# Fifteen stages on one core: constants loaded in the first norm, semaphores cleared in the next stage, output by chunk, rows of a partition side by side

## The chip, the cores and the metric

The kernel runs on one core of a Trainium2 chip. The metric is device time in microseconds (us) of one execution. The median of three runs of the kernel before is 4643.16 us (4641.54 to 4646.2).

## What is computed

4096 tokens of 128 features go through four layers, each with an attention (or a mixing) part and a feed-forward part. Every part adds to the same residual, and a layer norm stands ahead of each layer. Cut to its shape:

```python
def _layernorm(x, axis=-1, eps=1e-05):
    m = jnp.mean(x, axis=axis, keepdims=True)
    v = jnp.var(x, axis=axis, keepdims=True)
    return (x - m) / jnp.sqrt(v + eps)
...
act = jax.nn.silu(hpre)
y = jnp.einsum('tef,efh->teh', act, W2) + b2
out = jnp.einsum('te,teh->th', cw, y)
```

Layer 0 has softmax attention with 16 heads, a second attention block, and 8 dense experts. Layer 1 has attention with rotary tables and 8 experts of which each token takes 2. Layer 2 has linear attention and 8 experts with 2 for each token and a fixed capacity of 1024 rows for each expert. Layer 3 is a recurrent mixing and 64 small experts of which each token takes 8.

## The kernel before, in words

The residual `res_t` and the normed input `xn_t` stay in SBUF, features on the 128 partitions, tokens along the free side, in 8 chunks of 512 columns (`CH`, `BANK`). The program (`program`, L2950 on) is a row of 15 stages, each a function with one `Block`: n0, a0, b0, r0, e0, then n1, r1, a1, e1, then n2, r2, a2, e2, then n3, m3 (n is `layer_norm`, a an attention, b `whole_attention`, r a routing, e the experts, m `mixing_and_experts`). A `Block` gives each engine its own list of instructions and ends with a barrier: every engine drains, then all wait for one another. Within a block semaphores alone set the order.

Five places matter here.

The first block of `program` (L2955) is SP's alone: it issues the DMA of `avg`, of the eight chunks of `x` (L2961), and of 20 further constants (L2964). Norm n0 is the next block. Its tensor engine waits for `avg`, for each chunk of `x` and, ahead of the last chunk, for all the constants (`kept_in`).

At the end of every stage `pl.close()` (L39) opens one more `Block`, in which SP clears the stage's semaphores one by one (L45), and the barrier of that block has the line L41.

After the last stage a block of its own stores the output, one DMA of 2 MB, and waits for it (L3003, L3006).

The experts of layers 1 and 2 (`sorted_experts`, e1, and `slot_experts`, e2) read tokens that an earlier stage has scattered to DRAM by expert, 130 floats (520 bytes) to a row. Spans of 512 rows (e1) or 1024 rows (e2) are loaded with row t*128+p on partition p (L2753, L2513). The products go back to DRAM by indirect DMA, 128 rows of 512 bytes each, at the row numbers that travel with the tokens (L2865, L2642). In the end `y_in` is loaded in 16 DMAs of 256 KB (L2759, L2534), turned and added by the tensor engine (L2816, L2817; L2593, L2594), and added to the residual by the vector engine. A table `dest2` gives each token the row j*4096 + token.

In e2 SP's order is: weights, bias, a wait for the scatter, slots of expert 0 and 1, then the reloads. POOL (GpSimd) issues all the indirect DMAs.

Of the kernel before, what the change touches and what calls it, by code (L numbers as in the profile page):

```python
# [14 lines left out]
P = 128  # L15
# [7 lines left out]
class Place:  # L23


    def __init__(self, nc, ctx, stage):
        self.nc, self.ctx, self.stage, self.sems = nc, ctx, stage, []
# [7 lines left out]
    def sem(self, name):  # L35
        self.sems.append(self.ctx.enter_context(self.nc.semaphore(f"{self.stage}_{name}")))
# [25 lines left out]
def layer_norm(nc, stage, res_t, xn_t, avg, ident, bias, arrived=()):  # L62
# [6 lines left out]
    with ExitStack() as ctx:  # L69
# [87 lines left out]
def wide_attention(nc, stage, res_t, xn_t, w_d, w_out_d, ident, rowmask, scale, eps, clears, cleared):  # L157
# [41 lines left out]
    with ExitStack() as ctx:  # L199
# [319 lines left out]
def small_attention(nc, stage, res_t, xn_t, w, wo, ident, less, rope, w_moe_d, b_moe_d, split_d, split_out,  # L519
# [53 lines left out]
    with ExitStack() as ctx:  # L573
# [42 lines left out]
        with nc.Block() as block:  # L616
            @block.sync
            def _(eng):
                eng.wait_ge(filled, 3)
# [246 lines left out]
def whole_attention(nc, stage, res_t, xn_t, xp_t, w, bias, ident):  # L866
# [33 lines left out]
    with ExitStack() as ctx:  # L900
# [32 lines left out]
        with nc.Block() as block:  # L933
            @block.tensor
# [119 lines left out]
def linear_attention(nc, stage, res_t, xn_t, w_d, w_out_d, mask, ident, eps, rows, slot_of, slots_d, cleared, cleared_count, scattered):  # L1054
# [15 lines left out]
    with ExitStack() as ctx:  # L1070
# [49 lines left out]
        with nc.Block() as block:  # L1120
            @block.sync
            def _(eng):
                for p in range(PAIRS):
                    eng.dma_start(w[:, p, :], w_d[p, :, :]).then_inc(w_in, 16)
                    if p == 0:
                        eng.dma_start(wo[:, :, :], w_out_d).then_inc(const_in, 16)
                    eng.wait_ge(w_in, 16 * (p + 1))
                eng.wait_ge(const_in, CONSTS)

# [186 lines left out]
def route(nc, stage, x_t, w, bias, tri, ident, gates_d, E, top, norm_eps, squash, extra, extra_value, capacity):  # L1316
# [10 lines left out]
    with ExitStack() as ctx:  # L1327
# [37 lines left out]
        with nc.Block() as block:  # L1365
            @block.sync
            def _(eng):
                eng.wait_ge(turned_free, CH)
                eng.dma_start(gates_d, gates_t[:, :]).then_inc(stored, 16)
                eng.wait_ge(stored, 16)  # L1370
# [123 lines left out]
def mixing_and_experts(nc, stage, res_t, xn_t, d, gates_d, w_d, ident, w_route):  # L1494
# [49 lines left out]
    with ExitStack() as ctx:  # L1544
# [102 lines left out]
        with nc.Block() as block:  # L1647
            @block.sync
            def _(eng):
                for n in shape:  # L1650
                    eng.dma_start(const[n][tuple(slice(None) for _ in shape[n])], d[n + "3"]).then_inc(const_in, 16)
                eng.dma_start(w[:, :, :], w_d[0, :, :, :]).then_inc(w_in, 16)

# [6 lines left out]
                for n in range(UNITS):  # L1660
                    for pair in range(CH // 2):
# [394 lines left out]
def experts(nc, stage, res_t, x_t, w_d, bias_d, gates_d, units, act):  # L2056
# [42 lines left out]
    with ExitStack() as ctx:  # L2099
# [28 lines left out]
        with nc.Block() as block:  # L2128
            @block.sync
            def _(eng):  # L2130
# [9 lines left out]
                load_side(1, 1)  # L2140

# [131 lines left out]
def dispatch(nc, stage, xn_t, w, tri, ident, dest, base, rows, slot_of, norm_eps, sort, w_row):  # L2273
# [4 lines left out]
    with ExitStack() as ctx:  # L2278
# [34 lines left out]
        with nc.Block() as block:  # L2313
            @block.tensor
# [135 lines left out]
def slot_experts(nc, stage, res_t, slots_d, y_d, w_d, bias_d, ident, filled_sem, filled_count, sent):  # L2450
# [11 lines left out]
    with ExitStack() as ctx:  # L2462
# [44 lines left out]
        with nc.Block() as block:  # L2507
            @block.sync
            def _(eng):
                def load_slots(e):  # L2510
                    if e >= RING:
                        eng.wait_ge(gated, PER * (e - RING + 1))
                    eng.dma_start(slots[:, e % RING, :, :], slots_d[e * CAPACITY:(e + 1) * CAPACITY, :].rearrange("(t p) c -> p t c", p=P)).then_inc(slots_in[e % RING], 16)  # L2513
# [7 lines left out]
                eng.dma_start(bias[:, :, :], bias_d.rearrange("e p j -> p e j")).then_inc(const_in, 16)  # L2521
                eng.wait_ge(filled_sem, filled_count)
# [163 lines left out]
def sorted_experts(nc, stage, res_t, xn_t, slots_d, y_d, split_d, w_row, ident, filled_sem, filled_count, w_in, sent):  # L2686
# [9 lines left out]
    with ExitStack() as ctx:  # L2696
# [49 lines left out]
        with nc.Block() as block:  # L2746
            @block.sync
            def _(eng):
                eng.wait_ge(filled_sem, filled_count)
                for s in range(SORTED):  # L2750
                    if s >= SR:
                        eng.wait_ge(gated, s - SR + 1)
                    eng.dma_start(slots[:, s % SR, :, :], slots_d[s * BANK:(s + 1) * BANK, :].rearrange("(t p) c -> p t c", p=P)).then_inc(slots_in[s % SR], 16)  # L2753
                for r in range(2):
                    eng.wait_ge(sent[r], 16 * TILES * ((SORTED + 1 - r) // 2))
                for c in range(CH):
                    for j in range(2):
                        rows = slice(j * T + c * BANK, j * T + (c + 1) * BANK)
                        eng.dma_start(y_in[:, j, TILES * c:TILES * (c + 1), :], y_d[rows, :].rearrange("(t p) c -> p t c", p=P)).then_inc(y_loaded[c], 16)  # L2759
# [165 lines left out]
def program(nc, d, out):  # L2925

    gates = nc.dram_tensor("gates", (SMALL_EXPERTS + 2, T), F32, kind="Internal").ap()
    with ExitStack() as ctx:
# [20 lines left out]
                ("avg", "ident", "bias0", "rowmask0", "w_b0", "bias_b0", "w_g0", "b_g0", "tri", "dest2", "base2", "sort1", "w_g1", "w_qkv1",  # L2949
# [5 lines left out]
        with nc.Block() as block:  # L2955
            @block.sync
            def _(eng):
# [4 lines left out]
                for n in kept:  # L2962
                    if n != "avg":
                        eng.dma_start(kept[n][tuple(slice(None) for _ in d[n].shape)], d[n]).then_inc(kept_in, 16)  # L2964

        def in_parts(to, source, rows):
# [8 lines left out]
                   arrived=[([(avg_in, 16)] if c == 0 else []) + [(x_in[c], 16)] + ([(kept_in, 16 * (len(kept) - 1))] if c == CH - 1 else []) for c in range(CH)])  # L2975
# [25 lines left out]
        mixing_and_experts(nc, "m3", res_t, xn_t, d, gates, d["w_small"], kept["ident"], kept["w_route"])  # L3001

        with nc.Block() as block:  # L3003
            @block.sync
            def _(eng):
                eng.dma_start(out, res_t[:, :]).then_inc(stored, 16)  # L3006
                eng.wait_ge(stored, 16)


def lay_out(a):  # L3010
# [53 lines left out]
    def side_by_side(w, shared):  # L3064
# [22 lines left out]
        "w_g2": a["L2_ffn_gate_w"].T, "slots1": slots1, "sort1": sort1, "slots2": slots2, "dest2": ((np.arange(2) * T)[None, :, None] + np.arange(NT)[None, None] * P + p[:, :, None]).astype(np.float32),  # L3087
# [25 lines left out]
```

## Time and profile before

| | |
|---|---|
| median of the runs | 4643.16 us (4641.54 to 4646.2) |
| the profiled execution | 4609.9 us, with a span of 4607.5 us |
| TensorE busy | 4042.7 us, 88% of the span |
| VectorE busy | 3472.0 us, 75% |
| ScalarE busy | 2982.6 us, 65% |
| GpSimd busy | 2365.3 us, 51% |

Times are microseconds from the start of the span. PE is the tensor engine's matmul, PEld its weight load, DVE the vector engine, ACT the scalar engine, POOL GpSimd, SP the engine that issues most DMAs. A q behind an engine's name means its instruction queue: barriers, semaphore instructions and DMA issues, which aren't counted as busy. The profiled execution is 33 us shorter than the median of the runs; what lies around its span is 2.4 us.

### The profile page before, as it was taken

What the parts mean: (1) busy time and instruction counts of PE and PEld (TensorE: products, weight loads), DVE (VectorE), ACT (ScalarE), POOL (GpSimd) and SP (SyncE); (2) the same over time, 40 slices, a digit from 0 to 9 for tenths busy, and PEclk for the clock granted to TensorE, in tenths of its full rate; (3) what the DMA queues carried; (4) which work ended last, traced back from release to release, by engine and by line L of the source; (5) the groups of instructions that cost most, each with busy time, mean ns of one, the idle gap of its engine ahead of it and who ended that gap; (6) DMA issues with size and microseconds to landing.
All of it is one profiled execution on the core that took longest, in us unless ns stands there. A gap on an engine that the chain in (4) does not pass through costs nothing. (4 is left out here: it accounts for less than half of the span.)

```text
span 4607.5 us, 88670 instructions
## 1 busy us (share of the span) xinstructions
PE 4042.7 (88%) x34700; PEld 2257.5 (49%) x34700; DVE 3472.0 (75%) x4781; ACT 2982.6 (65%) x4498; POOL 2365.3 (51%) x1443
## 2 busy tenths in 40 slices
PE   5999999999998989985877777896888869999998
PEld 2666666666676644441111211344777443444443
DVE  5888888888884557756889898574777747888888
ACT  2777777777775459952677777782665726555564
POOL 2888888888884013320221110461666526666665
PEclk7999999999999989985899999897999979999999
DMA  2122212221120011100120100340000333333342
GB/s 81 45 51 57 57 42 51 57 57 48 48 48 1 1 70 46 69 1 28 62 73 31 43 22 13 109 138 26 13 14 13 102 92 94 95 100 99 95 105 75
DMA packets 139405, 261.47 MB, mean 57 GB/s; under 512 B 23908, under 2 KB 71908, under 8 KB 137388
## 3 DMA queue, kind: packets, MB, share of 16 engines
q1 hardware_dynamic: 123572, 215.01, 17.2%
q0 software_dynamic: 15424, 40.89, 2.6%
q8 instruction: 271, 4.44, 0.4%
q14 instruction: 138, 1.13, 0.1%
HBM read 170.31 MB, written 49.76 MB: 48 GB/s over the span
## 5 line engine op out<-in xcount | busy, mean ns | idle before, releaser
L513 POOL TENSOR_TENSOR a_prob_low<-a_prob_whole,a_prob_high 128x1024 f16<-128x1024 f32 x512 | 1084.9, 2130 | 276.6 <-ACT a_prob_high L403 276.6
L487 DVE TENSOR_REDUCE a_part_max<-a_top 128x2 f32<-128x1024 f32 x512 | 626.1, 1223 | 218.6 <-PE a_top L314 212.6
L400 ACT ACTIVATE a_prob_whole<-a_score 128x1024 f32<-128x1024 f32 x512 | 525.3, 1026 | 332.4 <-PE a_score L303 320.4
L757 ACT ACTIVATE a_prob<-a_score 128x512 f32<-128x512 f32 x1024 | 533.0, 603 | 260.7 <-PE a_score L701 260.7
L789 DVE TENSOR_REDUCE a_part_max<-a_side 128x2 f32<-128x1024 f32 x512 | 595.1, 1219 | 86.3 <-PE a_side L672 86.3
L1920 POOL TENSOR_TENSOR m_scaled<-m_acted,m_gate 128x512 f32<-128x512 f32 x264 | 433.2, 1649 | 271.5 <-DVE m_acted L2038 201.6
L403 ACT ACTIVATE a_prob_high<-a_score 128x1024 f16<-128x1024 f32 x512 | 521.9, 1019 | 0.0
L302 PE MATMUL a_score<-a_qa,a_ka 128*128 128x256 f16 x2048 | 476.2, 273 | 0.0
L303 PE MATMUL a_score<-a_qb,a_kb 128*128 128x256 f16 x2048 | 476.1, 273 | 0.0
L369 PE MATMUL a_o_ps<-a_v,a_prob_high 128*128 128x65 f16 x4096 | 428.1, 193 | 6.3 <-POOL a_prob_low L513 3.4
L371 PE MATMUL a_o_ps<-a_v,a_prob_high 128*128 128x64 f16 x4096 | 426.9, 194 | 0.0
L373 PE MATMUL a_o_ps<-a_v,a_prob_low 128*128 128x65 f16 x4096 | 424.5, 192 | 0.0
L369 PEld LDWEIGHTS a_o_ps<-a_v,a_prob_high 128*128 128x128 f16 x4096 | 376.0, 96 | 85.7 <-DVE a_tokens L473 35.3
L371 PEld LDWEIGHTS a_o_ps<-a_v,a_prob_high 128*128 128x128 f16 x4096 | 377.7, 97 | 26.9 <-issue 10.9
L373 PEld LDWEIGHTS a_o_ps<-a_v,a_prob_low 128*128 128x128 f16 x4096 | 377.9, 98 | 0.0
L1871 ACT ACTIVATE m_acted<-m_up_down 128x512 f32<-128x512 f32 x264 | 157.4, 597 | 320.7 <-PE m_up_down L1700 320.0
L701 PE MATMUL a_score<-a_qa,a_ka 32*128 32x512 f16 x1024 | 238.5, 400 | 91.0 <-ACT a_prob L757 88.4
L713 PE MATMUL a_o_ps<-a_prob,a_v 128*32 128x512 f32 x2048 | 290.4, 641 | 13.8 <-ACT a_raw L746 13.7
L701 PEld LDWEIGHTS a_score<-a_qa,a_ka 32*128 32x128 f16 x1024 | 60.4, 92 | 435.7 <-ACT a_prob L757 367.2
L2256 DVE TENSOR_TENSOR e_low<-e_whole,e_high 128x512 f16<-128x512 f32 x256 | 212.5, 842 | 80.3 <-ACT e_high L2214 79.9
L672 PE MATMUL a_side<-a_ka,a_qa 32*128 32x512 f16 x1024 | 217.9, 403 | 44.6 <-DVE a_part_max L789 22.3
L2044 DVE TENSOR_TENSOR m_lows<-m_scaled,m_high 128x512 f16<-128x512 f32 x264 | 241.8, 916 | 5.1 <-ACT m_high L1879 5.0
(440 smaller groups left out, 10378.0 us busy)
## 6 DMA issues: line engine op xcount, KB each, us to landing
m_gate<-gates SPq DMA_DIRECT2D x264, 256.0 KB, 5.1
a_ka<-a_nat_high_k SPq DMA_DIRECT2D x128, 128.0 KB, 2.4
e_gate<-gates SPq DMA_DIRECT2D x8, 2048.0 KB, 7.0
slots<-in_slots SPq DMA_DIRECT2D x19, 520.0 KB, 4.1
a_qa<-a_nat_high_q SPq DMA_DIRECT2D x64, 128.0 KB, 2.4
a_qa<-a_nat_low_q SPq DMA_DIRECT2D x64, 128.0 KB, 2.4
a_qb<-a_nat_high_q SPq DMA_DIRECT2D x64, 128.0 KB, 2.4
a_kb<-a_nat_low_k SPq DMA_DIRECT2D x64, 128.0 KB, 2.4
```

Source lines behind the costliest of these rows:

```text
L302: eng.matmul(score[:, e % 2, h, i, :], ka[:, r, h, keys], qa[:, r, h, qs], start=True, stop=False)
L303: mm = eng.matmul(score[:, e % 2, h, i, :], kb[:, r, h, keys], qb[:, r, h, qs], start=False, stop=True)
L369: eng.matmul(o_ps[:, at:at + V1], high, v[:, r, kt, h, 0:V1], start=(pair == 0 and i == 0 and h == 0 and t == 0), stop=False, skip_group_c ...
L371: eng.matmul(o_ps[:, at:at + DH], high, v[:, r, kt, h, V1 + 1:VW], start=False, stop=False, skip_group_check=True)
L373: mm = eng.matmul(o_ps[:, at:at + V1], low, v[:, r, kt, h, 0:V1], start=False, stop=last, skip_group_check=True)
L400: eng.activation(prob_whole[:, e % RING, :, :, :], score[:, e % 2, :, :, :], ACT.Exp, scale=scale)
L403: eng.activation(prob_high[:, e % RING, :, :, :], score[:, e % 2, :, :, :], ACT.Exp, scale=scale).then_inc(exp_done, 1)
L487: eng.tensor_reduce(part_max[:, i, c, :, qt % 4], top[:, :, :], AX.X, ALU.max).then_inc(max_done, 1)
L513: eng.tensor_tensor(prob_low[:, e % RING, :, :, :], prob_whole[:, e % RING, :, :, :], prob_high[:, e % RING, :, :, :], ALU.subtract).then_ ...
L757: eng.activation(prob[:, e % RING, h, :], score[:, step % SLOTS, :], ACT.Exp).then_inc(exp_done, 1)
L789: op = eng.tensor_reduce(part_max[:, qt // 4, c, 2 * pair:2 * pair + 2, 24 + qt], side, AX.X, ALU.max)
L1920: eng.tensor_tensor(scaled[:, s % SR, :], acted[:, s % AR, :], gate[:, g % 2, j, c % 2 * BANK:(c % 2 + 1) * BANK], ALU.mult).then_inc(scal ...
```

## The change

The kernel after differs in four ways.

1. The first block issues only `avg` and `x`. The 20 other constants are issued by SP inside the block of n0 (`loads`), with `bias0` ahead of `ident`.
2. `close()` opens no block. A stage's semaphores are kept until the next stage, whose SP clears them (`clear_before`): at the head of its list in the norms, b0, the routings and a1; behind the loads of weights in a0 and a2; behind the first loads in e0 and m3; behind weights and bias and ahead of the first slots in e2; behind the second load of slots in e1. The semaphores of m3 aren't cleared.
3. The last block is gone. In m3 SP stores each chunk of the output when its last two additions are done, and waits for all eight.
4. Loads of slots and of `y_in` take the rows of a partition side by side ("(p t) c" for "(t p) c"), and `dest2` gives token t*128+p the row p*32+t.

```diff
     def close(self):
-
-        with self.nc.Block() as block:
-            @block.sync
-            def _(eng):
-                for s in self.sems:
-                    eng.sem_clear(s)
+        if Place.before:
+            Place.before.held.close()
+        Place.before = self
...
+    def clear_before(self, eng):
+        for s in Place.before.sems if Place.before else ():
+            eng.sem_clear(s)
...
         with nc.Block() as block:
+            @block.sync
+            def _(eng):
+                pl.clear_before(eng)
+                for to, source in loads:
+                    eng.dma_start(to, source).then_inc(loads_in, 16)
...
+                for c in range(CH):
+                    at = slice(c * BANK, (c + 1) * BANK)
+                    eng.wait_ge(summed, (UNITS - 1) * CH + c + 1)
+                    eng.wait_ge(dve_done, dve_no["res", c])
+                    eng.dma_start(out_d[:, at], res_t[:, at]).then_inc(out_in, 16)
+                eng.wait_ge(out_in, 16 * CH)
...
-                    eng.dma_start(slots[:, e % RING, :, :], slots_d[e * CAPACITY:(e + 1) * CAPACITY, :].rearrange("(t p) c -> p t c", p=P)).then_inc(slots_in[e % RING], 16)
+                    eng.dma_start(slots[:, e % RING, :, :], slots_d[e * CAPACITY:(e + 1) * CAPACITY, :].rearrange("(p t) c -> p t c", p=P)).then_inc(slots_in[e % RING], 16)
...
                 eng.dma_start(bias[:, :, :], bias_d.rearrange("e p j -> p e j")).then_inc(const_in, 16)
+                pl.clear_before(eng)
                 eng.wait_ge(filled_sem, filled_count)
                 load_slots(0)
...
-                        rows = slice(j * T + c * BANK, j * T + (c + 1) * BANK)
-                        eng.dma_start(y_in[:, j, TILES * c:TILES * (c + 1), :], y_d[rows, :].rearrange("(t p) c -> p t c", p=P)).then_inc(y_loaded[c], 16)
+                        rows = y_d[j * T:(j + 1) * T, :].rearrange("(p t) c -> p t c", p=P)
+                        eng.dma_start(y_in[:, j, TILES * c:TILES * (c + 1), :], rows[:, TILES * c:TILES * (c + 1), :]).then_inc(y_loaded[c], 16)
...
-                for n in kept:
-                    if n != "avg":
-                        eng.dma_start(kept[n][tuple(slice(None) for _ in d[n].shape)], d[n]).then_inc(kept_in, 16)
...
-        with nc.Block() as block:
-            @block.sync
-            def _(eng):
-                eng.dma_start(out, res_t[:, :]).then_inc(stored, 16)
-                eng.wait_ge(stored, 16)
+        Place.before.held.close()
+        Place.before = None
+        pl.held.close()
```

## Rows read from the trace of the kernel before

**Rows 1.** The page's first part: busy time of each engine, share of the span, instructions.
```profile
PE 4042.7 (88%) x34700; PEld 2257.5 (49%) x34700; DVE 3472.0 (75%) x4781; ACT 2982.6 (65%) x4498; POOL 2365.3 (51%) x1443
```

**Rows 2.** Start, in order of time: start us, length us, engine, line.
```profile
1.20 3.74 SPq L2961 DMA_DIRECT2D all_res_t<-in_x  x8
...
14.21 0.43 SPq L2964 DMA_DIRECT2D all_kept_w_route<-in_w_route  x1
...
15.23 5.46 PE L102 MATMUL n_mean<-all_res_t,all_kept_avg 128*128 128x512 f32 x6 [15.23 <-PEq L2955]
...
28.38 1.10 PE L102 MATMUL n_mean<-all_res_t,all_kept_avg 128*128 128x512 f32 x2
```

**Rows 3.** Time from issue to landing of x's chunks, and of the last constant.
```profile
DMA to landing us min/median/max: 3.3/4.9/5.8
...
all_kept_w_route<-in_w_route SPq DMA_DIRECT2D x1, 32.0 KB, 4.0
```

**Rows 4.** SP's clears by line: all of them, and those of e2 and of m3.
```profile
L45 SPq EVENT_SEMAPHORE_RANGE_CLEAR  x242: 25/25/49, 47.7 to 4600.6; - x121
...
L45 SPq EVENT_SEMAPHORE_RANGE_CLEAR  x29: 25/25/30, 3730.2 to 3731.8; - x29
...
L45 SPq EVENT_SEMAPHORE_RANGE_CLEAR  x30: 25/30/49, 4598.5 to 4600.6; - x30
```

**Rows 5.** SP's release from e2's own barrier (L2507), then from the clearing block's (L41).
```profile
L2507 SPq EVENT_SEMAPHORE  x1: 17/17/17, 3730.1 to 3730.1; - x1
...
L41 SPq EVENT_SEMAPHORE  x1: 17/17/17, 3732.0 to 3732.0; - x1
```

**Rows 6.** Where clears go: a0's last first-unit load and first score; SP's wait in a1.
```profile
75.08 0.60 SPq L280 DMA_DIRECT2D a_kb<-a_nat_low_k  x1
...
101.96 0.40 PE L302 MATMUL a_score<-a_qa,a_ka 128*128 128x256 f16 x1
...
SPq L623 <- DVE a_fixed L768: 2.3, 1, 2.3
```

**Rows 7.** The end: last addition (chain of waits), last release of SP.
```profile
4597.55 0.69 DVE all_res_t L1941
...
L3003 SPq EVENT_SEMAPHORE  x1: 17/17/17, 4607.5 to 4607.5; - x1
```

**Rows 8.** Issues by line, median us to landing: stores of 256 KB from SBUF to DRAM.
```profile
a_planes<-a_low SPq DMA_DIRECT2D x8, 256.0 KB, 2.1
```

**Rows 9.** e2's start, in order of time.
```profile
3581.54 0.33 SPq L2518 DMA_DIRECT2D e_w<-in_w_moe  x1
...
3582.40 2.57 SPq L2513 DMA_DIRECT2D e_slots<-slots  x2
...
3588.40 1.09 PE L2550 MATMUL e_turned<-all_kept_ident,e_slots 128*128 128x128 f32 x4 [9.23 <-DMA e_slots<-slots]
```

**Rows 10.** e2's end, in order of time.
```profile
3706.46 0.96 POOL L2642 DMA_INDIRECT y<-e_y_s,e_dest  x1 [0.30 <-issue]
3708.77 11.87 SPq L2534 DMA_DIRECT2D e_y_in<-y  x16
3712.28 0.79 PE L2593 MATMUL e_back<-all_kept_ident,e_y_in 128*128 128x128 f32 x2 [19.52 <-DMA e_y_in<-y]
```

**Rows 11.** Tile e_y_in in e1: its loads, and the matmuls that read them.
```profile
L2816 PE MATMUL e_back<-all_kept_ident,e_y_in x64: 273/275/275, 3115.8 to 3129.8; 128*128 128x128 f32 x64
...
L2759 SPq DMA_DIRECT2D e_y_in<-y x16: 359/758/1103, 3096.9 to 3109.1; - x16
```

**Rows 12.** Waits in e1: us in total, times, longest.
```profile
DVE e_y_s L2904 <- DMA y<-e_y_s,e_dest: 31.8, 17, 2.9
```

**Rows 13.** Issues of the scatters, median us to landing.
```profile
y<-e_y_s,e_dest POOLq DMA_INDIRECT x156, 2.6
```

**Rows 14.** Stretches (PE, PEld, DVE, ACT, POOL busy; clock, DMA share, GB/s): x, a0's start.
```profile
7.00:8.00 1.00, 0.00 (x0) 0.00 (x0) 0.00 (x0) 0.00 (x0) 0.00 (x0) 1.00 1.02 377
...
51.00:106.00 55.00, 26.55 (x94) 8.49 (x94) 39.03 (x42) 10.24 (x14) 7.44 (x9) 0.50 0.36 91
```

More of the change, by code:

```diff
@@ L23 @@
 class Place:
+    before = None
     def __init__(self, nc, ctx, stage):
-        self.nc, self.ctx, self.stage, self.sems = nc, ctx, stage, []
+        self.nc, self.ctx, self.stage, self.sems, self.held = nc, ctx, stage, [], ExitStack()
     def sb(self, name, shape, dt=F32):
@@ L35, in sem @@
     def sem(self, name):
-        self.sems.append(self.ctx.enter_context(self.nc.semaphore(f"{self.stage}_{name}")))
+        self.sems.append(self.held.enter_context(self.nc.semaphore(f"{self.stage}_{name}")))
         return self.sems[-1]
+    def clear_before(self, eng):
+        for s in Place.before.sems if Place.before else ():
+            eng.sem_clear(s)
     def close(self):
-        with self.nc.Block() as block:
-            @block.sync
-            def _(eng):
-                for s in self.sems:
-                    eng.sem_clear(s)
+        if Place.before:
+            Place.before.held.close()
+        Place.before = self
 class Steps:
@@ L59, in wait, with layer_norm @@
         eng.wait_ge(self.sem, rnd * len(self.names) + self.place[name])
-def layer_norm(nc, stage, res_t, xn_t, avg, ident, bias, arrived=()):
+def layer_norm(nc, stage, res_t, xn_t, avg, ident, bias, arrived=(), loads=(), loads_in=None):
     LAG = 2
@@ L618, in _ @@
             def _(eng):
+                pl.clear_before(eng)
                 eng.wait_ge(filled, 3)
@@ L933, in whole_attention, with _ @@
         with nc.Block() as block:
+            @block.sync
+            def _(eng):
+                pl.clear_before(eng)
             @block.tensor
@@ L1128, in _ @@
                 eng.wait_ge(const_in, CONSTS)
+                pl.clear_before(eng)
             @block.tensor
@@ L1367, in _ @@
             def _(eng):
+                pl.clear_before(eng)
                 eng.wait_ge(turned_free, CH)
@@ L1491, in route, with mixing_and_experts @@
         pl.close()
-def mixing_and_experts(nc, stage, res_t, xn_t, d, gates_d, w_d, ident, w_route):
+def mixing_and_experts(nc, stage, res_t, xn_t, d, gates_d, w_d, ident, w_route, out_d, out_in):
     GROUPS = 4
@@ L1652, in _ @@
                 eng.dma_start(w[:, :, :], w_d[0, :, :, :]).then_inc(w_in, 16)
+                pl.clear_before(eng)
                 def store(pair):
@@ L2140, in _ @@
                 load_side(1, 1)
+                pl.clear_before(eng)
                 def reload(n, q):
@@ L2313, in dispatch, with _ @@
         with nc.Block() as block:
+            @block.sync
+            def _(eng):
+                pl.clear_before(eng)
             @block.tensor
@@ L2521, in _ @@
                 eng.dma_start(bias[:, :, :], bias_d.rearrange("e p j -> p e j")).then_inc(const_in, 16)
+                pl.clear_before(eng)
                 eng.wait_ge(filled_sem, filled_count)
@@ L2750, in _ @@
                 for s in range(SORTED):
+                    if s == 2:
+                        pl.clear_before(eng)
                     if s >= SR:
                         eng.wait_ge(gated, s - SR + 1)
-                    eng.dma_start(slots[:, s % SR, :, :], slots_d[s * BANK:(s + 1) * BANK, :].rearrange("(t p) c -> p t c", p=P)).then_inc(slots_in[s % SR], 16)
+                    eng.dma_start(slots[:, s % SR, :, :], slots_d[s * BANK:(s + 1) * BANK, :].rearrange("(p t) c -> p t c", p=P)).then_inc(slots_in[s % SR], 16)
                 for r in range(2):
@@ L2757, in _ @@
                     for j in range(2):
-                        rows = slice(j * T + c * BANK, j * T + (c + 1) * BANK)
-                        eng.dma_start(y_in[:, j, TILES * c:TILES * (c + 1), :], y_d[rows, :].rearrange("(t p) c -> p t c", p=P)).then_inc(y_loaded[c], 16)
+                        rows = y_d[j * T:(j + 1) * T, :].rearrange("(p t) c -> p t c", p=P)
+                        eng.dma_start(y_in[:, j, TILES * c:TILES * (c + 1), :], rows[:, TILES * c:TILES * (c + 1), :]).then_inc(y_loaded[c], 16)
             @block.tensor
@@ L2948, in program @@
         kept = {n: pl.sb("kept_" + n, list(d[n].shape)) for n in
-                ("avg", "ident", "bias0", "rowmask0", "w_b0", "bias_b0", "w_g0", "b_g0", "tri", "dest2", "base2", "sort1", "w_g1", "w_qkv1",
+                ("avg", "bias0", "ident", "rowmask0", "w_b0", "bias_b0", "w_g0", "b_g0", "tri", "dest2", "base2", "sort1", "w_g1", "w_qkv1",
                  "w_o1", "less1", "rope", "bias2", "w_g2", "mask2", "w_route")}
@@ L2974, in program @@
         layer_norm(nc, "n0", res_t, xn_t, kept["avg"], kept["ident"], kept["bias0"],
-                   arrived=[([(avg_in, 16)] if c == 0 else []) + [(x_in[c], 16)] + ([(kept_in, 16 * (len(kept) - 1))] if c == CH - 1 else []) for c in range(CH)])
+                   arrived=[([(avg_in, 16)] if c == 0 else []) + [(x_in[c], 16)] + ([(kept_in, 16 * (len(kept) - 1))] if c == CH - 1 else []) for c in range(CH)],
+                   loads=[(kept[n][tuple(slice(None) for _ in d[n].shape)], d[n]) for n in kept if n != "avg"], loads_in=kept_in)
         wide_attention(nc, "a0", res_t, xn_t, d["w_qkv0"], d["w_o0"], kept["ident"], kept["rowmask0"], scale=64 ** -0.5, eps=1e-10,
@@ L3000, in program @@
         layer_norm(nc, "n3", res_t, xn_t, kept["avg"], kept["ident"], None)
-        mixing_and_experts(nc, "m3", res_t, xn_t, d, gates, d["w_small"], kept["ident"], kept["w_route"])
-        with nc.Block() as block:
-            @block.sync
-            def _(eng):
-                eng.dma_start(out, res_t[:, :]).then_inc(stored, 16)
-                eng.wait_ge(stored, 16)
+        mixing_and_experts(nc, "m3", res_t, xn_t, d, gates, d["w_small"], kept["ident"], kept["w_route"], out, stored)
+        Place.before.held.close()
+        Place.before = None
+        pl.held.close()
 def lay_out(a):
```

2 lines of the change are left out of this document (1 added, 1 removed).

## The prediction

> **What bounds the kernel now.** I read the page's first part, then the order of time at every border between stages, then the waits of SP, because the change touches borders and little else. The tensor engine is busy for 88% of the span [rows 1], so only what lies on the chain of waits can shorten it. At a border all engines stand still, and what is removed there counts in full. The reader is to see four borders. At the start nobody works until SP has issued 28 loads [rows 2]. After each stage SP clears semaphores while all the others wait [rows 4, 5]. At the end a store of 2 MB runs alone [rows 7]. In e2 the tensor engine waits for its first slots and for the first rows of y_in [rows 9, 10].
>
> **Constants in the first norm.** The last constant's issue ends at 14.21 + 0.43 = 14.64, and the norm's first matmul starts 0.59 later, at 15.23 [rows 2]. After the change the block ends with x, at 1.20 + 3.74 = 4.94, so the matmul starts at 5.53: 9.7 us earlier. What is late next? Chunk 0 lands 3.3 us after its issue at the soonest row, at 4.5. The eighth chunk, issued at about 4.5 and 5.8 at most on its way, lands at 10.3, and its matmul comes at 28.38 - 9.7 = 18.7 [rows 2, 3]. That matmul also waits for all constants. SP starts on them at about 5.4 in place of 4.94, so the last is issued at about 14.7 and lands 4.0 later, at 18.7 [rows 3]. This is a tie. With x's longest time of 5.8 it would be 1.8 us late. I take 9.7, bounds 7.9 and 9.7. Nothing else stands on SP's queue in the norm.
>
> **Clearing blocks.** There are 242 clears, 30 of them m3's [rows 4], so 212 lie between stages, in 14 blocks. In e2's block 29 clears start over 1.6 us, 0.057 each; from the release of the stage's barrier to that of the clearing block are 1.9 us, and the remaining 0.2 to 0.3 are drain and barrier [rows 4, 5]. 212 x 0.057 + 14 x 0.25 = 15.6 us, all of it on the path, since no engine works there.
>
> The same clears now run on SP beside a stage. In norms, routings and b0, SP has nothing urgent. In a1 they take 8 x 0.057 = 0.5 us ahead of a wait of 2.3 us [rows 6]. In a0 they come ahead of the loads for the first scores, the last of which is issued at 75.08, while the first score comes at 101.96 [rows 6]: 11 x 0.057 = 0.6 us hidden. In a2 nothing of SP follows them. In e0 and m3 they stand behind the first loads, and what follows are reloads and stores that wait for other engines; I take nothing, and where that cover is gone it is 0.5 to 0.6 us each. In e1, 17 clears (1 us) delay the third span of slots, which is used after two whole spans. Only in e2 do they stand on the path: the 20 of a2, 1.1 us, ahead of the slots that the tensor engine waits for [rows 9].
>
> **Output by chunk.** The last addition ends at 4597.55 + 0.69 = 4598.24, the last release is at 4607.5 [rows 7]. Between them lie m3's clears, a barrier and the whole store. After the change only the last chunk's store follows. A store of the same form, 256 KB with 2 KB from each partition, lands in 2.1 us [rows 8]; the upper bound is 4.9, what a chunk of x took amid seven others [rows 3]. With 0.1 to see the semaphore and 0.3 for the last barrier the end is 4600.7: gain 6.8, down to 4.0. The other seven stores run earlier, on a queue with no work behind it. By the Trainium skill, "DMA: Bandwidth & Descriptors", section Bandwidth, transfers should be batched to 1 MiB or more, and this cuts one of 2 MB into eight; it bears on bytes per second, and here only the last piece is on the path, so the sum would not follow it.
>
> **Rows side by side.** In e2 two loads of slots take 2.57 us to issue (1.28 each, runs of 520 bytes), one of weights with runs of 4 KB takes 0.33, and from the first issue to the first turn pass 6.0 us [rows 9]. With runs of 4160 bytes I take a landing of 4.9, the middle row of x [rows 3]: 1.1 gained, and the 1.1 of the clears pays for it. So 0, bounds -1.1 and +1.6 (the 3.3 of x). At e2's end 16 loads are issued in 11.87 us, 0.74 each, and the matmul starts 3.5 us after the first [rows 10]. With 2 KB runs, as x has, an issue takes 3.74 / 8 = 0.47 [rows 2]. The pair is on its way 0.5 us sooner; I take 0.5, bounds 0 and 1. In e1 all of y_in is issued by 3109.1 and used from 3115.8 [rows 11]: nothing. The scatters keep their number and size, and I take them as unchanged.
>
> Sum: 9.7 + 15.6 + 6.8 + 0 + 0.5 = 32.6 us. The profiled execution would go from 4609.9 to 4577.3. The median of the runs is 33 us above it; the edits act on single moments of every execution, so I subtract the same: 4643.2 - 32.6 = 4610.6. By the bounds the gain is 26.4 to 35, that is 4608 to 4617.
>
> **Rivals.** *The clearing blocks were a cover.* If the engines used the 1.1 us of a block (15.6 / 14) to get ready for the next stage, that time comes back: gain 17.0, time 4626. For it speaks that every engine goes to another list there. Against it: the border without a clearing block, ahead of n0, takes 0.59 us from SP's last issue to the matmul [rows 2]. The Trainium skill, "Runtime: NRT & Kernel Launch", section Instruction fetch mechanics, says that a taken branch out of the present window stalls for a fetch. By that rule this case is the one that happens, and 4626 its time; the trace so far speaks against it. Chance 0.10.
>
> *The tensor clock.* From 51 to 106 us the granted clock is 0.50 (1.2 GHz) with PE busy for 26.55 us [rows 14]. The stretch follows the norm, where PE waits for others. If after the shift it is shorter or longer, PE's part can change by up to 26.55 / 2 = 13 us. Other borders have smaller ones. Better: 4598 to 4608, chance 0.10. Worse: 4617 to 4624, chance 0.08.
>
> *The scattered rows land later (slower).* Neighbouring tokens of an expert now lie at 16 KB steps, not at 512 bytes. DVE already waits 31.8 us in e1 for such landings [rows 12]. POOL issues four per span at 0.96 + 0.30 = 1.26 us [rows 10], 5.0 in all; a landing of 2.6 [rows 13] and a multiplication of 0.7 fit in with 1.7 to spare. From a landing of 4.3 on, each further microsecond costs one in each of 39 spans (23 in e1, 16 in e2). Beyond 4.3 + 42 / 39 = 5.4 the kernel is over 0.2% slower; at 5.5, 1.2 x 39 = 47 us, time 4657. Against it: x is read at the same 16 KB steps at 377 GB/s [rows 14]. [...] Chance 0.05.
>
> *It doesn't do what it says.* If the constants hold up the last chunk by all of the 9.7 us and the borders give back 15.6, 7.3 remain: 4636, within 0.2%. Chance 0.05.
>
> **The numbers.** The forecast itself (4608 to 4617) has 0.62, and its time is 4610.6. 4602 to 4626 takes in the forecast, the worse clock, most of the cover rival in its partial forms, and half of the better clock: about 0.84. A change under 0.2% (9.3 us) is about what a measurement of this kernel can't tell from none. Faster: 0.62 + 0.10 + 0.10 + 0.08 = 0.90. Same 0.05, slower 0.05.
>
> **What would show it.** Right: the first matmul at 5.5, the last chunk's at 18.7 to 20; no line L41; next stage's first work within 0.2 us of the release; last release 2.4 us behind the last addition; one slots issue at 0.4; y_in issues at 0.5. Wrong: idle time at the head of stages that names no releaser; a matmul of n0 waiting for constants; a scatter landing above 4 us; borders as predicted, but a sum of stages that has changed, which would be the clock.

## The result, and the profile after

| | us, median | runs | range |
|---|---|---|---|
| before, runs of the same comparison | 4641.54 | 5 | 4629.96 to 4646.2 |
| after | 4603.1 | 5 | 4599.24 to 4611.19 |

The ratio is 0.9923, 95% interval 0.991 to 0.9936: 38 us faster, with the forecast at 4610.6 and its range at 4608 to 4617. The profiled execution of after took 4609.92 us, its span is 4608.0. That of before took 4609.9, with a span of 4607.5. Laid side by side the two profiles say that nothing was gained. The first thing to settle is therefore which of them stands for what.

The page of after, first part, answers to [rows 1]:

```profile
PE 4038.5 (88%) x34698; PEld 2252.7 (49%) x34700; DVE 3471.0 (75%) x4781; ACT 2976.9 (65%) x4498; POOL 2359.2 (51%) x1443
```

The busy times are the same: the change took idle time away, or moved it. The start of after, in order of time (start us, length us, engine, line), answers to [rows 2]:

```profile
1.19 3.75 SPq L2992 DMA_DIRECT2D all_res_t<-in_x  x8
...
5.53 1.19 PE L110 MATMUL n_mean<-all_res_t,all_kept_avg 128*128 128x512 f32 x1 [5.53 <-PEq L2986]
...
14.26 0.43 SPq L100 DMA_DIRECT2D all_kept_w_route<-in_w_route  x1
...
18.38 1.72 PE L110 MATMUL n_mean<-all_res_t,all_kept_avg 128*128 128x512 f32 x2 [0.78 <-DMA all_kept_w_route<-in_w_route]
```

The first matmul is at 5.53, 9.7 us earlier. The last chunk's names the last constant as what it waited for, 0.78 us. The end of after, in order of time, and SP's last release, answer to [rows 7]:

```profile
4604.84 0.69 DVE L1964 TENSOR_TENSOR all_res_t<-all_res_t,m_out 128x512 f32<-128x512 f32 x1 [2.31 <-PE m_out L1723]
4605.56 0.33 SPq L1698 DMA_DIRECT2D out_t<-all_res_t  x1
...
L1663 SPq EVENT_SEMAPHORE  x1: 17/17/17, 4607.9 to 4607.9; - x1
```

The last store is issued 0.03 us after the addition (4605.53), and the kernel ends 2.4 us after it. In before that distance was 9.3. So the removed pieces are gone from this profile, and its span is still no shorter. Where did the 32 us of these pieces come back? I took the time of each stage from SP's release at the end of its block to the next release, clearing blocks apart:

| us | before | after |
|---|---|---|
| start | 15.0 | 5.3 |
| n0 | 32.6 | 34.2 |
| a0, b0, r0, e0 | 1955.8 | 1956.0 |
| n1, r1, a1 | 903.5 | 896.9 |
| e1 | 216.4 | 245.0 |
| n2, r2, a2 | 445.4 | 443.6 |
| e2 | 148.7 | 160.5 |
| n3 | 26.7 | 27.6 |
| m3 | 838.9 | 839.0 with the stores |
| clearing blocks, whole store | 24.5 | 0 |

e1 and e2 are 40 us longer. They are also the only stages whose rows the change lays out anew. Waits in e1 of after (us in total, times, longest), and the last line of the view of tile y, in which I first looked for the scatters' landing, answer to [rows 12, 13]:

```profile
ACT e_whole L2873 <- PE e_hidden L2798: 48.3, 24, 6.5
POOL y L2896 <- DVE e_y_s L2935: 45.5, 7, 18.4
DVE e_low L2922 <- ACT e_high L2876: 43.9, 48, 3.9
...
DMA to landing us min/median/max: 2.8/5.6/6.8
```

A landing of 5.6 us, and a longer e1, is what the rival "the scattered rows land later" asked for, and it is how I read the line at first. One thing speaks against it: the wait of VectorE for a landing, 31.8 us in [rows 12], is absent. What grew are waits between TensorE, ScalarE and VectorE.

### The profile page after: what moved, and what is told of

It is laid out like the page before. It is cut to its first block and busy times, and to the rows that moved or that the text cites. A ratio compares the mean times of both kernels' runs of the same rounds, so it can differ in the third digit from the quotient of the medians.

```text
span 4608.0 us, 88475 instructions
## 1 busy us (share of the span) xinstructions
PE 4038.5 (88%) x34698; PEld 2252.7 (49%) x34700; DVE 3471.0 (75%) x4781; ACT 2976.9 (65%) x4498; POOL 2359.2 (51%) x1443
```

## The experiments

Two explanations stood open. In the first, the new order of rows makes e1 and e2 longer. In the second, something outside the kernel does, and it differs between the profile of before and the runs. Each comparison ran on one chip, with its own runs of before; the chips bear the numbers 8, 6, 9 and 13, and each served in one comparison only.

**The orders of rows undone, on chip 8** (before 4636.01 us, 4631.69 to 4642.1, 7 runs). The changed kernel again, no edit:

> The changed kernel as it is, once more, as the reference for its variants. Its first profile had the same span as that of before (4608.0 to 4607.5 us) though its runs were 38 us shorter: e1 took 245.0 us (216.4 before) and e2 160.5 (148.6 before), with scatters that landed in 5.7 us (median) where 2.8 stood before. Theory L (the new order of rows slows the scatters, always): e1 is 240 us or more again, the landing above 5 us, the time 4600 to 4610. Rival V (e1 and e2 vary from execution to execution whatever the order is, and the one profile of before was a lucky one): e1 may lie anywhere from 215 to 245, and the time within 4570 to 4610.

Then the order of y undone, in the loads and in the table of destinations:

```diff
-rows = y_d[j * T:(j + 1) * T, :].rearrange("(p t) c -> p t c", p=P)
-eng.dma_start(y_in[:, j, TILES * c:TILES * (c + 1), :], rows[:, TILES * c:TILES * (c + 1), :]).then_inc(y_loaded[c], 16)
+rows = slice(j * T + c * BANK, j * T + (c + 1) * BANK)
+eng.dma_start(y_in[:, j, TILES * c:TILES * (c + 1), :], y_d[rows, :].rearrange("(t p) c -> p t c", p=P)).then_inc(y_loaded[c], 16)
...
-np.arange(NT)[None, None] + p[:, :, None] * NT
+np.arange(NT)[None, None] * P + p[:, :, None]
```

> The changed kernel, with the rows of y in their old order (token number) and y_in loaded as before; slots still side by side. Theory L-y (the 16 KB steps between a scatter's rows make the landing long): the landing falls back to 2.8 us, e1 to 217 and e2 to 149 us, and the time to 40 us below the changed kernel. Theory L-slots (what counts is which slots one scatter takes): no change, e1 stays at 240 or more. Rival V: no change beyond scatter, ratio to the changed kernel within 0.3%.

Then the order of the slots undone, then both:

```diff
-slots_d[...].rearrange("(p t) c -> p t c", p=P)
+slots_d[...].rearrange("(t p) c -> p t c", p=P)
```

> The changed kernel, with slots loaded in the old order (row t*128+p on partition p); rows of y and y_in in the new order. Theory L-slots: e1 falls to 217 us, the time by 40 us. Theory L-y: e1 stays at 240 or more, the time stays. The slots' loads themselves have short runs again: their issue in e2 1.28 us each in place of 0.4, and e2's start within 1 us of the changed kernel's.

> The changed kernel without any of the new orders of rows: only the three edits on borders, constants and output are left. By the prediction's sum without its last term (0.5 us) it should be 32 us faster than the kernel before and within 1 us of the changed kernel. Theory L (either part): e1 217, e2 149 us, 40 us faster than the changed kernel, that is 70 us faster than before by the runs. Rival V: the same time as the changed kernel within 0.3%, e1 anywhere from 215 to 245.

| | us | ratio to before, 95% | e1 us | median landing, loads of y_in, us |
|---|---|---|---|---|
| after again | 4597.04 | 0.9914 (0.9897 to 0.993) | 244.3 | 5.4 |
| y old | 4600.06 | 0.9922 (0.9905 to 0.9938) | 239.8 | 4.6 |
| slots old | 4592.31 | 0.9909 (0.9892 to 0.9926) | 238.4 | 5.6 |
| both old | 4599.41 | 0.9922 (0.9906 to 0.9939) | 236.7 | 4.7 |

The expectations speak of the scatters' landing. The number of 5.6 isn't that: tile y's view takes the loads of y_in in, and in these profiles the scatters themselves have no landing. The issues by line show it, for after again:

```profile
e_y_in<-y SPq DMA_DIRECT2D x32, 256.0 KB, 5.4
...
y<-e_y_s,e_dest POOLq DMA_INDIRECT x156
```

So I took the scatters' packets from the trace, 16 for each of e1's 92. The last one ends 1.94 to 2.16 us after the issue (median) in the six profiles of the long e1, and 2.29 to 2.31 in the seven of the short one that scatter. The rows don't land late. With both orders as before, e1 is still 20 us longer than the 216.4 of before's profile. So the new orders are not what made it long. Between the four, e1 differs by up to 8 us, but the whole times follow no order and their intervals overlap. The orders together are worth less than these runs can tell: after again and both old have medians 2.4 us apart, with four runs each, and their ranges overlap (4592.38 to 4601.15, 4595.56 to 4605.03).

**The other parts undone one by one, on chip 6** (before 4606.14 us, 4598.19 to 4614.97, 19 runs). The kernel before itself, for its profile, no edit:

> The kernel before, once more, for a second profile. Four profiles with either order of rows gave e1 237 to 245 us and e2 150 to 160, and no time that the orders tell apart, while the first profile of before had 216.4 and 148.6. Theory V (the first profile of before was of an unusually short e1): e1 is 235 to 245 us, a scatter lands in 4.6 us or more, the span is 4630 to 4640. Rival E (the edits on borders lengthen e1, for instance by clears behind the second load or by other semaphores): e1 is 216 again, the landing 2.8, the span 4607 to 4612, and the runs of before are longer than that for a reason outside the trace.

The changed kernel with a clearing block after each stage again:

```diff
     def clear_before(self, eng):
-        for s in Place.before.sems if Place.before else ():
-            eng.sem_clear(s)
+        pass
...
     def close(self):
...
+        with self.nc.Block() as block:
+            @block.sync
+            def _(eng):
+                for s in self.sems:
+                    eng.sem_clear(s)
```

> The changed kernel with the clearing blocks back (a block behind each stage, m3's too), constants, output and orders of rows as changed. By the prediction's sum 15.6 us slower than the changed kernel between stages and 2 us at the end: 4597 + 18 = 4615. Rival (the blocks were a cover for getting ready for the next stage): within 3 us of the changed kernel.

With the constants in the first block again:

```diff
                     eng.dma_start(res_t[:, at], d["x"][:, at]).then_inc(x_in[c], 16)
+                for n in kept:
+                    if n != "avg":
+                        eng.dma_start(kept[n][tuple(slice(None) for _ in d[n].shape)], d[n]).then_inc(kept_in, 16)
```

> The changed kernel with all constants issued in the first block again. By the sum, with the measured wait of the last chunk, 8 to 9.7 us slower than the changed kernel: 4597 + 9 = 4606; first matmul at 15.2, n0 32.6 us. Rival (tensor clock: the shift moves a0's slow stretch): a difference of under 4 or over 14 us, and it lies in a0.

With the output as one store in a block of its own:

```diff
-                for c in range(CH):
-                    ...
-                    eng.dma_start(out_d[:, at], res_t[:, at]).then_inc(out_in, 16)
-                eng.wait_ge(out_in, 16 * CH)
...
+        with nc.Block() as block:
+            @block.sync
+            def _(eng):
+                eng.dma_start(out, res_t[:, :]).then_inc(stored, 16)
+                eng.wait_ge(stored, 16)
```

> The changed kernel with one store of 2 MB in a block of its own behind m3, without m3's clears. The last addition to the end was 9.3 us before, 2.4 of it the clearing block; so 6.7 to 6.9 us, against 2.4 for the chunks: 4.4 us slower than the changed kernel, 4601. Rival (the chunk stores disturb m3's last unit and cost what they save): within 1 us.

Here before ran in 4606, not 4636 to 4642, and e1 took 216.7 us in its profile. I then wanted the changed kernel's own time on such a chip. It came to **chip 9** (before 4607.73 us, 4599.54 to 4610.32, 13 runs), with two others:

> The kernel before once more, for a profile of it beside the others of this call. The theory (the first expert stage is long or short by the chip a kernel runs on, not by the kernel): where the comparison runs of before stand at 4630 to 4645 us, this profile shows the stage at 237 to 245 us instead of 216 and the last expert stage at 151; where they stand at 4600 to 4612, 216 and 149. The rival (the changed kernel makes the stage long, by where its instructions or buffers lie): 216 in this profile also where the comparison stands at 4630 to 4645.

> The changed kernel itself, same call. The theory: the difference to before is the same on either chip, 33 to 39 us, so 4595 to 4607 where before stands at 4630 to 4645, with the first expert stage at 237 to 245 us; 4567 to 4574 where before stands at 4606, with that stage at 216 to 218, since the clearing blocks cost some 18, the constants some 10 and the output 4 to 5 there. The rival (the changed kernel makes the stage long): a difference that shrinks by 20 us or more on one of the chips, and 237 to 245 us in this profile whatever before shows.

> The changed kernel, where the first expert stage writes its rows of y in the order in which they are made, by plain transfers from GpSimd's queue, instead of scattering them by index (so the rows stand in other places than the reference wants; the count and size of the writes is the same). If the indirect scatters are what slows the handoffs between the engines in the long form of the stage, it takes 218 us or less on a chip where z2 has 237 to 245. If something else there does it (the indirect loads of the weights, the traffic itself), it stays at 235 or more. On a chip where z2 has 216 to 218, this takes 200 to 218: VectorE waits 32.6 us in all for the landing of y there, beside TensorE's work for the most part.

The edit of the third. It leaves the rows of y in the order in which they are made, so its output isn't the reference's:

```diff
-eng.indirect_dma_start(y_d, bass.IndirectOffsetOnAxis(dest[:, s, t:t + 1], 0),
-                       y_s[:, s % 2, t, :], None).then_inc(sent[s % 2], 16)
+eng.dma_start(y_d[s * BANK + t * P:s * BANK + (t + 1) * P, :], y_s[:, s % 2, t, :]).then_inc(sent[s % 2], 16)
```

| | us | ratio to before, 95% | start | e1 | clearing blocks | last addition to end |
|---|---|---|---|---|---|---|
| before again (6) | 4604.55 | 0.9997 (0.9987 to 1.0007) | 14.9 | 216.7 | 17.8 | |
| clearing blocks back (6) | 4595.56 | 0.9976 (0.9966 to 0.9985) | 5.4 | 218.2 | 17.9 | |
| constants first (6) | 4579.99 | 0.9945 (0.9928 to 0.9961) | 15.0 | 217.7 | 0 | |
| whole store (6) | 4573.91 | 0.9938 (0.9922 to 0.9955) | 5.3 | 216.5 | 0 | 6.9 |
| before again (9) | 4604.51 | 0.9997 (0.9987 to 1.0007) | 15.0 | 217.1 | 17.8 | 9.2 |
| after again (9) | 4567.14 | 0.9919 (0.9902 to 0.9937) | 5.3 | 216.8 | 0 | 2.4 |
| plain writes (9) | 4564.46 | 0.9907 (0.989 to 0.9923) | 5.3 | 204.7 | 0 | |

The changed kernel has the short e1 too, on chip 9. With the long e1 its time is 4597 to 4603, with the short one 4567; before stands at 4636 to 4642 in the one kind of comparison and at 4606 to 4608 in the other. The change brings the same everywhere: 0.9923, 0.9914 and 0.9919. So the profile of before, at 4609.9, came from the kind with the short stage, and the runs of 4641 to 4646 beside it from the other. That before has the long e1 there is inferred from its 30 us; no profile of it was taken on such a chip.

The two forms of e1 are best read in the same kernel. First chip 9, the changed kernel, waits in e1 (us in total, times, longest):

```profile
DVE e_y_s L2935 <- DMA y<-e_y_s,e_dest: 32.2, 17, 2.3
...
ACT e_whole L2873 <- PE e_hidden L2798: 25.2, 32, 7.7
...
POOL y L2896 <- DVE e_y_s L2935: 19.1, 1, 19.1
```

Then chip 8, the same kernel, its waits in e1:

```profile
POOL y L2896 <- DVE e_y_s L2935: 49.9, 8, 18.5
ACT e_whole L2873 <- PE e_hidden L2798: 44.6, 23, 6.6
DVE e_low L2922 <- ACT e_high L2876: 36.1, 50, 3.6
...
DVE e_x_high L2909 <- remote: 24.3, 6, 5.9
```

"remote" is a releaser that the profile can't place; it occurs in e1 of the long form only. A stretch of that stage on chip 8, in order of time, shows what such a wait is:

```profile
2970.61 0.69 DVE L2922 TENSOR_TENSOR e_low<-e_whole,e_high 128x512 f16<-128x512 f32 x1
...
2971.07 0.38 PE L2798 MATMUL e_hidden<-e_x_high,e_w 128*128 128x512 f16 x1
...
2971.93 0.60 PE L2805 MATMUL e_turned<-all_kept_ident,e_slots 128*128 128x128 f32 x4
...
2973.58 0.69 ACT L2873 ACTIVATE e_whole<-e_hidden,e_w 128x512 f32<-128x512 f32 x1 [3.01 <-remote]
2974.17 0.68 ACT L2876 ACTIVATE e_high<-e_hidden,e_w 128x512 f16<-128x512 f32 x1
2974.88 0.69 DVE L2922 TENSOR_TENSOR e_low<-e_whole,e_high 128x512 f16<-128x512 f32 x1 [3.58 <-issue]
2974.99 0.38 PE L2796 MATMUL e_hidden<-e_x_high,e_w 128*128 128x512 f16 x1 [2.45 <-issue]
```

ScalarE waits for two things here. The product was done at 2971.45 and VectorE's subtraction, which frees the buffer, at 2971.30; ScalarE starts 2.1 us later. The trace's record of the semaphore that this product raises stands at 2973.56, just ahead of that start. TensorE then has nothing to do for 2.45 us. The work is the same; the word between engines comes late. Counted from the traces over all 124 such steps of e1, ScalarE starts over 0.3 us after the last end of what it waits for in 18 to 25 steps in each of the six long profiles (37 to 52 us in sum, 6.5 at most in one), and in none in each of the eight short ones.

**A deeper buffer for the scatters, on chip 13** (before 4640.07 us, 4632.93 to 4651.47, 9 runs). The plain writes had taken VectorE's wait for the landing away and 12 us of e1 with it. The same with the rows in their right places would be a faster kernel:

```diff
-y_s = pl.sb("y_s", [P, 2, TILES, P])
+y_s = pl.sb("y_s", [P, 4, TILES, P])
...
-if s >= 2:
-    eng.wait_ge(sent[s % 2], 16 * TILES * (s // 2))
+if s >= 4:
+    eng.wait_ge(sent[s % 4], 16 * TILES * (s // 4))
```

(the scatters, their semaphores and SP's final waits go by four in the same way)

> The changed kernel, where the rows that the first expert stage scatters lie in four buffers in turn instead of two. With two, VectorE waits 32.2 us in all in 17 places of that stage for rows to land before it may fill the buffer again, and with plain writes the wait was gone and the stage 12.1 us shorter (204.7 us against 216.8). If that wait is what the 12 us were, they come here too with the rows where the reference wants them: the stage at 203 to 208 us and the whole some 9 to 13 us below the changed kernel, so 4554 to 4559 us where before stands at 4606, 4582 to 4590 where it stands at 4636 to 4642. The rival (the plain writes saved GpSimd's time for the indices, 0.98 us each against 0.54, and not the wait): GpSimd becomes the wait in its place, and the stage stays at 214 to 217 us. A weaker form of the theory for a chip where the stage took 237 to 245: the wait is not what makes it long there, and it stays at 230 or more.

It came to a chip with the long form: 4603.85 us (4594.36 to 4610.96), ratio 0.9918 (0.9899 to 0.9936), e1 246.9. That is the changed kernel's own ratio. No wait for a landing was left, but in the long form there was none to take away: e1 of the changed kernel on chip 8 has no such wait either. So the theory's weaker form held, that the wait isn't what makes e1 long there, and this run says nothing on what four buffers gain. Whether they bring 9 to 13 us where e1 is short was not measured. For the plain writes the median itself was only 2.7 us below the changed kernel's on chip 9, with overlapping intervals: in its profile a1 and e2, which have nothing to do with them, took 837.0 us against 831.2 and 153.0 against 148.3.

## Why the prediction was right, step by step

The time was within 7.5 us of the forecast, and the gain 38 us instead of 32.6 (37.4 on chip 9 between the two kernels' own medians, 39.0 on chip 8 against before's runs). That is more than the bounds allowed: the sum gave 26.4 to 35 us and a time of 4608 to 4617, and the median of 4603.1 lies 5 us below that, in the wider band of 4602 to 4626. The interval of the ratio is a gain of 30 to 42 us, which still reaches into the bounds, but three comparisons have their medians above them. The terms held one by one, as follows; what lies above their sum has no term of its own in the prediction but the clock rival's. The cleanest measure of the steps is chip 9, two profiled executions with e1 alike: spans 4602.2 and 4566.4, 35.8 us apart.

**Constants.** Forecast 9.7; measured 9.7 at the first matmul between the first two profiles (15.23 to 5.53) and 9.8 on chip 9 (15.29 to 5.53). The tie at the last chunk was a tie: forecast 18.7, measured 18.38 with a wait of 0.78 us in after, 18.55 on chip 9. n0 took 31.3 to 34.5 us in the ten profiles with the early start and 30.7 to 32.6 in the four with the late one, so up to a microsecond may have come back there. In the profile of after, where n0 is 1.6 us longer than in before, the granted clock is 0.52 from the last chunk's product to the next group (18.3 to 29.1 us), against 0.65 in before (28.3 to 37.1). With the constants first (chip 6) the ratio is 0.9945, with the whole change 0.9919 (chip 9): 12 us, and the ends of the intervals allow -4 to 27. The loads ahead of the first work are 29, not 28 as the prediction says: `avg`, eight chunks and 20 constants.

**Clearing blocks.** Forecast 15.6 for the 14 between stages; all 15 took 17.8 us, and m3's took 2.4 of it from release to release, so 15.4. The clears are now where they cost nothing. On chip 9, the changed kernel, SP's clears by line (duration min/median/max in ns, first and last start):

```profile
L42 SPq EVENT_SEMAPHORE_RANGE_CLEAR  x212: 25/30/49, 57.1 to 3735.2; - x106
```

The rival "the blocks were a cover" is refuted by the border from a0 to b0 in after, in order of time:

```profile
1427.74 0.69 DVE L469 TENSOR_TENSOR all_res_t<-all_res_t,a_side 128x512 f32<-128x512 f32 x1 [3.63 <-PE a_side L360]
1428.72 0.50 PEld L959 LDWEIGHTS b_wide<-all_xn_t,all_kept_w_b 128*128 128x128 f32 x2 [2.60 <-issue]
1428.76 5.19 PE L959 MATMUL b_wide<-all_xn_t,all_kept_w_b 128*128 128x512 f32 x8 [1.05 <-PEq L268]
```

The last addition of a0 ends at 1428.43, the first matmul of b0 starts 0.33 us later. The other borders agree: in before and after alike, the first work of a stage starts 0.08 to 0.10 us after SP's release at 12 of the 14, 0.77 at e1 and 4.1 to 4.2 at e2. The Trainium skill ("Runtime: NRT & Kernel Launch", section Instruction fetch mechanics) has it that a taken branch out of the present window stalls for a fetch. At this border no stall of the 1.1 us that the rival asked for is seen; whether b0's list lay outside the window the trace doesn't tell. The experiment with the blocks put back went the other way than a cover would: 0.9976 against 0.9919 is 26 us (13 to 38 by the ends of the intervals), more than the 17.9 in the blocks. In its profile the other 11.6 us are spread over the stages (n3 2.9, n2 2.4, eight others by 0.6 to 1.5, n0 and n1 shorter by 1.1). One profile can't tell that from their usual spread, so a cost of the blocks beyond their own time stays open.

**Output.** Forecast 6.8. On chip 9, the end of before, then of after:

```profile
4592.18 0.69 DVE L1941 TENSOR_TENSOR all_res_t<-all_res_t,m_out 128x512 f32<-128x512 f32 x1 [2.31 <-PE m_out L1700]
...
4595.49 0.35 SPq L3006 DMA_DIRECT2D out_t<-all_res_t  x1
...
L3003 SPq EVENT_SEMAPHORE  x1: 17/17/17, 4602.1 to 4602.1; - x1
```

```profile
4563.28 0.69 DVE L1964 TENSOR_TENSOR all_res_t<-all_res_t,m_out 128x512 f32<-128x512 f32 x1 [1.84 <-PE m_out L1723]
4563.99 0.33 SPq L1698 DMA_DIRECT2D out_t<-all_res_t  x1
...
L1663 SPq EVENT_SEMAPHORE  x1: 17/17/17, 4566.3 to 4566.3; - x1
```

9.2 us from the addition's end to the last release became 2.4: 6.8. The kernel with the whole store and no clears stands at 6.9, so the store gave 4.5 and m3's clears the rest. By [rows 8] the last piece should land in 2.1; the median of the eight is 2.1 on chip 9. By the runs the store is worth 9 us (ratio 0.9938 against 0.9919, the ends of the intervals allow -7 to 24). The three parts put back one by one (clearing blocks, constants, store) come to 47 us by the runs and to 17.9 + 9.7 + 4.5 = 32.1 by their profiles: the runs show the gain of the whole, and the size of a part rests on the profiles.

**Rows.** e2's start: forecast 0. On chip 9 the first turn came 6.4 us after the issue of the weights in before (3576.18) and 7.1 in after. In order of time, before, then after:

```profile
3577.04 2.50 SPq L2513 DMA_DIRECT2D e_slots<-slots  x2
...
3582.54 1.09 PE L2550 MATMUL e_turned<-all_kept_ident,e_slots 128*128 128x128 f32 x4 [8.73 <-DMA e_slots<-slots]
```

```profile
3552.11 0.33 SPq L2546 DMA_DIRECT2D e_w<-in_w_moe  x1
3552.49 0.43 SPq L2549 DMA_DIRECT2D e_bias<-in_b_moe  x1
3554.12 0.81 SPq L2541 DMA_DIRECT2D e_slots<-slots  x2
...
3559.17 1.09 PE L2579 MATMUL e_turned<-all_kept_ident,e_slots 128*128 128x128 f32 x4 [8.28 <-DMA e_slots<-slots]
```

The clears hold the slots up by 1.20 us (from 3552.92 to 3554.12); the forecast was 1.1. The two slots are issued in 0.81 instead of 2.50, but the first is in use only 0.5 us sooner after its issue (5.05 against 5.50), not 1.1. That makes 0.7 lost in this pair, inside the bounds, but it can't be told from none: from the issue of the weights to the first turn the three profiles of before take 6.4, 6.9 and 7.4 us, those of the changed kernel and its variants 5.9 to 7.5. At e2's end the sixteen loads of y take 8.34 us to issue instead of 11.87 [rows 10], and the matmul still starts 3.83 after the first (3.51 before): the shorter issue didn't bring the pair sooner, so the 0.5 was not there. It is the order that does this: the matmul starts 3.8 to 4.1 us after the first issue in every profile with the new order of y and 3.5 to 3.6 in every one with the old, the changed kernels with y old and both old among them. These loads take longer each: 5.6 us to landing (median) in e2 on chip 9 against 4.4 in before. Whether by their closer issue or by where the rows lie no run separates. e2 as a whole took 148.4 and 148.3.

**The clock.** A small part of this rival came true, on the good side. The last addition of m3 starts 834.9 to 835.9 us after the stage's release in the changed kernels of chips 6 and 9, and 837.5 to 838.2 in before. The stage's first 10 us on chip 9 (busy us of PE, PEld, DVE, ACT, POOL with counts; clock, DMA share, GB/s), before and then after:

```profile
3754.00:3764.00 10.00, 9.87 (x56) 9.90 (x56) 0.12 (x2) 3.07 (x4) 1.18 (x2) 0.61 0.78 244
```

```profile
3727.80:3737.80 10.00, 7.33 (x64) 7.22 (x64) 0.12 (x2) 3.67 (x5) 1.18 (x2) 1.00 0.78 246
```

Of the same routing products 56 take 9.87 us at a granted clock of 0.61, and 64 take 7.33 at 1.00 (2.4 GHz). But this opening isn't what made m3 shorter: the kernel with the clearing blocks back opens like before (55 products in 10 us at 0.61), and its last addition comes 834.9 us after the release all the same. From 140 to 180 us after the release the clock is 0.91 in before and 0.96 both in that kernel and in the changed one of chip 9. How much of the 2.7 us is the clock's, and what moves its dips, isn't shown.

**What the sum leaves.** The terms as measured on chip 9 are 9.8 + 15.4 + 6.8 and nothing for the rows, 32.0 us, and the spans differ by 35.8. Of the 3.8 left over 2.7 are m3's. The rest is the net of the other stages, with n0 2.1 us longer, a2 2.0 and a1 1.2 shorter, which vary by as much between profiles of kernels in which they are the same.

**The step that was luck.** I subtracted what the profile showed from a median 33 us above it, on the ground that the edits act at single moments of every execution. The ground was right: both kinds of comparison give the same ratio. But I didn't ask what the 33 us were. They were, as far as the profiles show, two stages in another form. Had the change touched e1's chain of engines, its price read from the short form would not have been that of the runs.

**The rival of the late landings** named a landing above 4 us as its sign, and a microsecond for each span from 4.3 on. The sign was there (5.6), and e1 was 28.6 us longer, nearly what the formula gives for its 23 spans (1.3 x 23 = 30). It was a coincidence of a number that belongs to other transfers. The packets end no later than in before, the old order has an e1 of 236.7 on the same chip, and with four buffers, which would absorb a late landing, e1 is 246.9.

## What to carry to other kernels

A border at which every engine stands still is worth its full length, and can be priced by counting its instructions: 212 clears in 14 blocks, 29 loads ahead of the first work and a store after the last came out within 0.2 us each, by the profiles. Before a profile of one execution is compared with another, compare the time of the executions with the medians, and the stages the change doesn't touch with each other: here two spans equal to 0.5 us hid a gain of 38 us. When a rival's sign appears in the profile of after, look whose number it is, and undo the part it blames before believing it.

## What the runs showed of the hardware

One kernel has two times: with before, 4604 to 4608 us on chips 6 and 9, 4636 and 4640 on chips 8 and 13. Within a comparison the runs keep to one of them, but each chip served in one comparison only, so that it is the chip, and not the hour or what else ran there, isn't shown. In the changed kernel and its variants e1, the stage with indirect loads and scatters on GpSimd's queue, takes 216 to 218 us on the first two and 237 to 247 on the others. The mean granted clock of the execution is 0.95 in both; within e1 it is 0.97 to 0.98 in the short form and 0.93 to 0.97 in the long; e0, the stage with the same products but loads that need no indices, takes 345 to 347 on all. On the long chips the scatters' packets end as early as on the others, but words between TensorE, ScalarE and VectorE come up to 6.5 us late at times. What delays them, and what differs between the comparisons, stays open: the run with plain writes, meant to tell whether the indirect transfers do it, came to a chip with the short form. There it showed e1 about 12 us shorter without the scatters even so (204.7 against 216.8, one profile each).
